# Perceiver block on one NeuronCore: the first batch's fill reordered, with matmuls on constants ahead of it

## The reference

```python
x = x + cross_attention(layernorm(x), ctx, ctx)      # 16 heads of 32, ctx is 8 x 512 x 512
x = x + linear_attention(layernorm(x))               # feature map elu+1, 128 features
x = x + moe(layernorm(x))                            # 16 experts, 8 tokens each per batch, and a shared one
```

```python
qh = (q @ Wq + bq).reshape(b, n, H, HD)
kh = (k @ Wk + bk).reshape(b, k.shape[1], H, HD)
vh = (v @ Wv + bv).reshape(b, v.shape[1], H, HD)
attn = jax.nn.softmax(scale * einsum("blhe,bshe->bhls", qh, kh), axis=-1)
out = einsum("bhls,bshd->blhd", attn, vh).reshape(b, n, H * HD) @ Wo + bo
```

## Time and profile before

| | |
|---|---|
| median of 3 runs | 668.30 us |
| lowest and highest | 667.94, 669.22 us |
| profiled execution, its own time | 668.04 us |
| its span, first to last instruction | 665.2 us |
| instructions in the span | 10401 |

### The profile page before, as it was taken

One profiled execution on the slowest core, in us unless ns is written; L12 is line 12 of the kernel. 1 busy time (PEld: TensorE's weight loads), 2 busy tenths in 40 slices (PEclk: granted clock), 3 DMA queues, 4 the chain that ended last, 5 costly groups with the idle time before them and its releaser, 6 DMA issues.

```text
span 665.2 us, 10401 instructions
## 1 busy us (share of the span) xinstructions
PE 638.2 (96%) x4216; PEld 414.6 (62%) x4216; DVE 312.3 (47%) x643; ACT 255.3 (38%) x488; POOL 34.8 (5%) x38
## 2 busy tenths in 40 slices
PE   6989999999999999999999988999999999999997
PEld 5767777777878786678978564444444434443433
DVE  5965636444453615755778675423223222323123
ACT  5645636444544536546684342111121212211210
POOL 0400000000000001535000000000000000000000
PEclk9999999999999999999999989999999999999999
DMA  8211010110340000031239724989999999999971
GB/s 314 82 64 64 2 65 2 63 53 12 125 194 0 2 1 2 1 111 34 98 108 399 283 97 165 379 356 396 391 414 414 403 403 401 394 379 397 372 282 70
DMA packets 14347, 129.55 MB, mean 195 GB/s; under 512 B 2720, under 2 KB 2848, under 8 KB 6240
## 3 DMA queue, kind: packets, MB, share of 16 engines
q1 hardware_dynamic: 12576, 127.15, 48.9%
q10 hardware_dynamic: 1728, 1.77, 0.8%
HBM read 125.90 MB, written 1.05 MB: 191 GB/s over the span
## 4 chain that ended last, share of the span: by engine, by line
PE 75%; DVE 9%; DMA 9%; ACT 4%; issue 2%; SPq 1%; DVEq 0%; ACTq 0%
PE ps L1209 23%; PE ps L1496 14%; DMA w_u<-in_wu 8%; PE ps L1533 7%; PE ps L1403 5%; PE ps L1506 4%; PE ps L1279 4%; PE ps L1546 3%; PE ps L1255 3%; PE ps L1290 2%; PE ps L1320 2%; PE ps L1450 2%; PE ps L1352 2%; PE ps L1462 1%; PE ps L1522 1%
## 5 line engine op out<-in xcount | busy, mean ns | idle before, releaser
L1496 PE MATMUL ps<-w_u,x_slot 128*64 128x512 f32 x256 | 58.1, 595 | 2.0 <-DMA w_u<-in_wu 2.0
L1496 PE MATMUL ps<-w_g,x_slot 128*64 128x512 f32 x256 | 58.1, 595 | 0.8 <-ACT x_slot L780 0.8
L1533 PE MATMUL ps<-w_d,hid_T 128*64 128x512 f32 x256 | 58.1, 596 | 0.7 <-issue 0.7
L582 ACT ACTIVATE probs<-ps,neg_max 128x512 f32<-128x512 f32 x64 | 43.5, 688 | 39.1 <-DVE neg_max L899 39.1
L742 ACT ACTIVATE hid<-ps 128x512 f32<-128x512 f32 x24 | 14.4, 598 | 102.5 <-PE ps L1496 76.8
L1209 PE MATMUL ps<-wv_hi,ctx_hi 128*128 128x512 f32 x128 | 51.6, 403 | 0.0
L1209 PE MATMUL ps<-wv_lo,ctx_hi 128*128 128x512 f32 x128 | 50.0, 390 | 0.0
L1209 PE MATMUL ps<-wv_hi,ctx_lo 128*128 128x512 f32 x128 | 49.8, 389 | 0.0
L879 DVE COPY probs_T<-ps 128x512 f32<-128x512 f32 x28 | 19.4, 692 | 64.8 <-PE ps L1279 64.8
L899 DVE TENSOR_REDUCE neg_max<-ps 128x1 f32<-128x512 f32 x64 | 39.7, 682 | 18.4 <-PE ps L1255 18.3
L1071 DVE TENSOR_TENSOR hid<-hid,ps 128x512 f32<-128x512 f32 x24 | 16.5, 687 | 65.8 <-PE ps L1496 36.2
(11 more groups left out here) (246 smaller groups left out, 1185.2 us busy)
## 6 DMA issues: line engine op xcount, KB each, us to landing
w_u<-in_wu SPq DMA_DIRECT2D x16, 2048.0 KB, 16.4
w_d<-in_wd SPq DMA_DIRECT2D x16, 2048.0 KB, 12.8
w_g<-in_wg SPq DMA_DIRECT2D x16, 2048.0 KB, 13.7
ctx_raw<-in_ctx SPq DMA_DIRECT2D x7, 1024.0 KB, 4.8
w_qkv<-in_wqkv SPq DMA_DIRECT2D x1, 3072.0 KB, 15.3
ws_g<-in_wsg SPq DMA_DIRECT2D x1, 2048.0 KB, 7.8
ws_u<-in_wsu SPq DMA_DIRECT2D x1, 2048.0 KB, 7.9
ws_d<-in_wsd SPq DMA_DIRECT2D x1, 2048.0 KB, 21.3
```

What stands on the lines that cost most here:

```text
L582: act.activation(probs[:, p, :], bank(SCORE[p]), ACT.Exp, bias=neg_max[:, p:p + 1], scale=1.0, accum_out=row_sum[:, p:p + 1]).then_inc(exp ...
L1496: ins = pe.matmul(ps[64 * fh:64 * (fh + 1), dst, :], x_slot[:, e, dt, :], weights[e % 2][:, dt, BANK * fh:BANK * (fh + 1)], start=(dt == 0 ...
L1533: ins = pe.matmul(ps[64 * fh:64 * (fh + 1), 6 + side(n), :], hid_T[:, side(n), j, 64 * fh:64 * (fh + 1)], w_d[e % 2][:, KT * fh + j, :], s ...
```

## The change

- TensorE begins with 34 matmuls (`WARM`) of 128 columns on the constant `ones`, into a bank that is not read before it is written anew. They wait for the first four constants only.
- `first_keys` goes part by part: for each depth tile high x high of all four key tiles, then low weights x high context, then high weights x low context, each behind its own wait.
- `ln_transpose` moves into the middle of value tile 3.
- `project_q` goes part by part over all depth tiles, high x high first; tile 0 uses bank 6 instead of 3.
- TensorE's order becomes: query tiles 0, 1, 2, first score group, query tile 3, key tile 0 of batch 1, second score group; `step(1)` then starts with key tile 1.
- The counter `q_done` becomes two, one for each engine that takes query tiles out.
- ScalarE: a square root on a constant at the very start; key outputs ahead of the first square roots; high parts of the query weights in two halves, with value output 0 between; value output 1 behind the last roots; query output 2 ahead of the exponents.
- GpSimd's first row bias waits in addition for the second score group of batch 1 (`score_ps` 4).

```diff
@@ -278,7 +278,7 @@
         w_hi, w_split, wv_split, wq_split = sem("w_hi"), sem("w_split"), sem("wv_split"), sem("wq_split")
         ctx_hi_done, ctx_split = sem("ctx_hi_done"), sem("ctx_split")
         k_ps, k_done, v_ps, v_done = sem("k_ps"), sem("k_done"), sem("v_ps"), sem("v_done")
-        q_ps, q_done, bias_scaled = sem("q_ps"), sem("q_done"), sem("bias_scaled")
+        q_ps, q_done, bias_scaled = sem("q_ps"), [sem("q_done_act"), sem("q_done_dve")], sem("bias_scaled")
         score_ps, max_done, exp_done, inv_done, prob_done = (
             sem("score_ps"), sem("max_done"), sem("exp_done"), sem("inv_done"), sem("prob_done"))
         pT_ps = sem("pT_ps")
@@ -316,7 +316,8 @@
         SCORE = (5, 6, 7, 2, 5, 6, 7, 3)
         GROUP = PAIRS // 2
         FIRST_K = 4
-        Q_BANK = (3, 4, 0, 1)
+        Q_BANK = (6, 4, 0, 1)
+        WARM = 34
 
         LN_BANK, RES_BANK = 2, ((7, 0, 1, 7), (0, 1, 2, 3))
         ROW_BANK = 4
@@ -494,6 +495,7 @@
                     pool.tensor_tensor(x[:, t, :], x[:, t, :], row_bias[:], ALU.add).then_inc(xbias_done, 1)
 
             pool.wait_ge(rows_in, 16)
+            pool.wait_ge(score_ps, 4)
             add_row_bias(0, bo_rows)
 
             def weights_low(parts):
@@ -570,7 +572,7 @@
             def q_out(ht):
                 act.wait_ge(q_ps, ht + 1)
                 act.activation(q_T[:, ht, :], bank(Q_BANK[ht]), ACT.Identity,
-                               bias=bias_q_scaled[:, ht:ht + 1], scale=HD ** -0.5).then_inc(q_done, 1)
+                               bias=bias_q_scaled[:, ht:ht + 1], scale=HD ** -0.5).then_inc(q_done[0], 1)
 
             def probs_T_out(b, tiles=range(KT)):
                 for ht in tiles:
@@ -589,30 +591,35 @@
                         if i >= 2:
                             v_out(b, 2 * g + i - 2)
 
+            def query_weights_high(tiles):
+                act.wait_ge(wq_in, 16)
+                for dt in tiles:
+                    act.copy(wq_hi[:, dt], wq_raw[:, dt]).then_inc(w_hi, 1)
+
+            act.wait_ge(consts, 4)
+            act.activation(newton[:, 0:1], iota_p[:], ACT.Sqrt)
             first_high()
             act.wait_ge(wv_in, 16)
             for dt in range(KT):
                 act.copy(wv_hi[:, dt], wv_raw[:, dt]).then_inc(w_hi, 1)
             act.wait_ge(bias_in, 48)
-            ln_std(0, (0, 1))
-            act.wait_ge(wq_in, 16)
-            for dt in range(KT):
-                act.copy(wq_hi[:, dt], wq_raw[:, dt]).then_inc(w_hi, 1)
             for ht in range(KT):
                 k_out(0, ht, first=True)
+            ln_std(0, (0, 1))
+            query_weights_high((0, 1))
+            act.wait_ge(wv_split, KT)
+            v_out(0, 0)
+            query_weights_high((2, 3))
             ln_std(0, (2, 3))
-            act.wait_ge(wv_split, KT)
-            for st in range(NS - 1):
-                v_out(0, st)
+            v_out(0, 1)
+            v_out(0, 2)
             xn_high()
             v_out(0, NS - 1)
             ctx_high(1, 1)
             act.wait_ge(bias_scaled, 1)
             q_out(0)
-            for p in range(GROUP - 1):
-                exponent(0, p)
             q_out(2)
-            for p in range(GROUP - 1, PAIRS):
+            for p in range(PAIRS):
                 exponent(0, p)
 
             def step(b, par, more=True):
@@ -871,7 +878,7 @@
             def q_out(ht):
                 dve.wait_ge(q_ps, ht + 1)
                 dve.tensor_scalar(q_T[:, ht, :], bank(Q_BANK[ht]), bias_q[:, ht:ht + 1], HD ** -0.5,
-                                  ALU.add, ALU.mult).then_inc(q_done, 1)
+                                  ALU.add, ALU.mult).then_inc(q_done[1], 1)
 
             def probs_T_out(b, tiles=range(KT)):
                 for ht in tiles:
@@ -1201,10 +1208,12 @@
                     ins = pe.transpose(ps[:, t, P * dt:P * (dt + 1)], xn_lin[:, t, P * dt:P * (dt + 1)], ident[:])
                 ins.then_inc(xnT_ps, 1)
 
-            def product3(dst, lhs, rhs):
+            def product3(dst, lhs, rhs, behind=None):
 
                 (l_hi, l_lo), (r_hi, r_lo) = lhs, rhs
                 for dt in range(KT):
+                    if behind and dt == KT // 2:
+                        behind()
                     for i, (a, c) in enumerate(((l_hi, r_hi), (l_hi, r_lo), (l_lo, r_hi))):
                         ins = pe.matmul(dst, a(dt), c(dt), start=(dt == 0 and i == 0), stop=(dt == KT - 1 and i == 2))
                 return ins
@@ -1212,15 +1221,14 @@
             def first_keys():
 
                 for dt in range(KT):
-                    pe.wait_ge(w_split, dt + 1)
-                    pe.wait_ge(ctx_split, dt + 1)
-                    for ht in range(KT):
-                        cols = slice(P * ht, P * (ht + 1))
-                        for i, (w, c) in enumerate(((wk_hi, ctx_hi), (wk_hi, ctx_lo), (wk_lo, ctx_hi))):
+                    for i, (w, c) in enumerate(((wk_hi, ctx_hi), (wk_lo, ctx_hi), (wk_hi, ctx_lo))):
+                        pe.wait_ge(*((ctx_hi_done, dt + 1), (w_split, dt + 1), (ctx_split, dt + 1))[i])
+                        for ht in range(KT):
+                            cols = slice(P * ht, P * (ht + 1))
                             ins = pe.matmul(bank(FIRST_K + ht), w[:, dt, cols], c[:, 0, dt, :],
                                             start=(dt == 0 and i == 0), stop=(dt == KT - 1 and i == 2))
-                        if dt == KT - 1:
-                            ins.then_inc(k_ps, 1)
+                            if dt == KT - 1 and i == 2:
+                                ins.then_inc(k_ps, 1)
 
             def project_k(b, par, tiles=range(KT)):
                 pe.wait_ge(ctx_split, b + KT)
@@ -1234,7 +1242,7 @@
                              (lambda dt: wk_hi[:, dt, cols], lambda dt: wk_lo[:, dt, cols]),
                              (lambda dt: ctx_hi[:, par, dt, :], lambda dt: ctx_lo[:, par, dt, :])).then_inc(k_ps, 1)
 
-            def project_v(b, par, st, first=False):
+            def project_v(b, par, st, first=False, behind=None):
                 if st >= 2:
                     pe.wait_ge(v_done, b * NS + st - 1)
                 elif first:
@@ -1244,7 +1252,7 @@
                 cols = slice(P * st, P * (st + 1))
                 product3(bank(PROJ[st % 2]),
                          (lambda dt: ctx_hi[:, par, dt, cols], lambda dt: ctx_lo[:, par, dt, cols]),
-                         (lambda dt: wv_hi[:, dt, :], lambda dt: wv_lo[:, dt, :])).then_inc(v_ps, 1)
+                         (lambda dt: wv_hi[:, dt, :], lambda dt: wv_lo[:, dt, :]), behind).then_inc(v_ps, 1)
 
             def score_group(b, g):
 
@@ -1302,40 +1310,43 @@
                 attend(b, 2)
                 attend(b, 3)
 
+            pe.wait_ge(consts, 4)
+            for _ in range(WARM):
+                pe.matmul(ps[:, LN_BANK, 0:P], ones[:], ones[:], start=True, stop=True)
             pe.wait_ge(consts, HPT + 5)
             first_keys()
             for st in range(NS - 1):
                 project_v(0, 0, st, first=True)
             pe.wait_ge(k_done, 2)
-            ln_transpose()
-            project_v(0, 0, NS - 1, first=True)
+            project_v(0, 0, NS - 1, first=True, behind=ln_transpose)
 
             def project_q(ht):
                 cols = slice(P * ht, P * (ht + 1))
-                for dt in range(KT):
-                    if ht == 0:
-                        pe.wait_ge(wq_split, dt + 1)
-                        pe.wait_ge(xn_split, dt + 1)
-                    for i, (w, c) in enumerate(((wq_hi, xn_hi), (wq_hi, xn_lo_cross), (wq_lo, xn_hi))):
+                for i, (w, c) in enumerate(((wq_hi, xn_hi), (wq_lo, xn_hi), (wq_hi, xn_lo_cross))):
+                    for dt in range(KT):
+                        if ht == 0:
+                            pe.wait_ge(*((xn_hi_done, dt + 1), (wq_split, dt + 1), (xn_split, dt + 1))[i])
                         ins = pe.matmul(bank(Q_BANK[ht]), w[:, dt, cols], c[:, dt, :],
                                         start=(dt == 0 and i == 0), stop=(dt == KT - 1 and i == 2))
                 ins.then_inc(q_ps, 1)
 
-            pe.wait_ge(xn_split, 2)
+            pe.wait_ge(k_done, KT)
             project_q(0)
             project_q(1)
-            pe.wait_ge(k_done, KT)
-            pe.wait_ge(q_done, 2)
-            score_group(0, 0)
             pe.wait_ge(v_done, NS)
             project_q(2)
+            for done in q_done:
+                pe.wait_ge(done, 1)
+            score_group(0, 0)
+            pe.wait_ge(q_done[0], 2)
             project_q(3)
-            pe.wait_ge(q_done, KT)
+            project_k(1, 1, (0,))
+            pe.wait_ge(q_done[1], 2)
             pe.wait_ge(exp_done, GROUP - 1)
             score_group(0, 1)
 
             def step(b, par):
-                project_k(b, par, range(KT - 1))
+                project_k(b, par, range(b == 1, KT - 1))
                 probs_transpose(b - 1, 0)
                 probs_transpose(b - 1, 1)
```

## The result

The changed kernel takes **671.45 us** (median of 5 runs, 670.98 to 672.67) against 667.94 for the kernel before in the same comparison (666.49 to 669.22, 5 runs). The ratio is 1.0064, 95% interval 1.0047 to 1.008: slower by 0.6%, where 667.3 was forecast and "faster" had the highest chance (0.48). The profiled execution's span is 670.6 us, 5.4 more than before; it was the second slowest of the five (672.55), so its trace shows somewhat more loss than the median does.

The account below looks back on a forecast made before the run. TensorE, busy 96% of the span, was taken as the bound, with time to win in batch 0's fill. Fill gain -2.5 plus clock fall +1.5 gave -1.0: 668.04 to 667.0 profiled, median 0.3 higher, 667.3; range 664.9 to 669.4.

Parts of the forecast that it names:

- The first keys: Batch 0's key products at the start: after the warm-up they end at 17.4 instead of 18.55, -1.15 us.
- if the clock rises 3.5 us in, as before: TensorE's warm-up: 19 matmuls at 0.178 us, then 15 at 0.11, 5.0 us in all, ending at 6.5.
- Rival D: Slower: the warm-up matmuls do not raise the clock, keys end at 20.2, 670.1 us; chance 0.14.
- the chain from the keys' end on: Fill from value tile 0 (17.4) to batch 1's third key tile: 52.1 against 54.57, a gain of 2.5 us.
- the gap and its price: TensorE before batch 1's third key tile: 3.3 us idle, then a clock fall costing +1.5 us.
- rival B: The clock holds over the idle gap before batch 1's third key tile, 665.8 us; chance 0.24.
- The row that the prediction drew on: Granted clock 0.50 at 389 us after idles of 1.01 and 0.77 us, used to expect a fall after 3.3 us.
- delays the scores by the rest: Key tile 0 before the second scores: of its 2.73 us, 0.84 covers idle and the rest delays those scores.
- the row bias: GpSimd's additions moved away: VectorE's low query weights take 2.5 us, not 5.69; additions near 72 us cost nothing.
- the Exp table load: ScalarE's 1.28 us load moves behind query output 2; first exponent 0.4 us late, second score group's wait hidden.
- Rival C: Short warm-up ending at 5.2, keys end at 16.1, value weights bind; 666.0 us with the clock fall, 664.5 without; chance 0.10.

Follow-up runs that it names:

- run 1: The changed kernel without the 34 warm-up matmuls: 667.45 us, ratio 0.9994 to the kernel before.
- Run 8: The kernel before with only GpSimd's row bias held back until the second scores of batch 1: 666.97 us, ratio 0.9976.
- run 2: The changed kernel with 8 matmuls of 512 columns on constants in place of the 34 of 128: 665.78 us, ratio 0.997 to the kernel before.
- run 3: The kernel before with only the 34 warm-up matmuls put ahead: 669.91 us, ratio 1.0033.
- run 4: The changed kernel with the 3 MB weight load held back until batch 5's scores are done: 670.37 us, ratio 1.0041 to the kernel before.
- Run 6: The changed kernel with 8 wide warm-up matmuls and 13 unread matmuls in the gap before batch 1's third key tile: 664.22 us, ratio 0.9944.
- run 5: The changed kernel with 8 wide warm-up matmuls and batch 1's key tile 0 behind the second scores: 664.22 us, ratio 0.9947 to the kernel before.
- run 9: The changed kernel with 8 wide warm-up matmuls, key tile 0 behind second scores, 16 transposes in the gap, query output 3 before two normalisations: 662.49 us, ratio 0.9931.
- run 10: The kernel before with only 8 warm-up matmuls of 512 columns put ahead: 667.69 us, ratio 1.0001.

## Why the prediction was wrong, point by point

**The step that failed is the first term,** "The first keys: -1.15". Its price of 0.178 us for a warm-up matmul at the low clock was taken from four transposes; it was 0.215, which makes 1.2 us over the 34. And its condition, "if the clock rises 3.5 us in, as before", did not hold: it rose only after 512-column key products had run, which makes another 2.5: 0.9 in the warm-up itself and 1.6 in the slow key products. Value tile 0 came at 21.12 instead of 17.4, an error of 3.7 us. The "as before" was also the short end of what the kernel does: in runs 1 and 8, without a warm-up, the clock rose some 5.5 us behind the first product. Rival D had the outcome, that these matmuls do not raise the clock; it was given 0.14 and its warm-up was priced 1.0 us too short, with keys at 20.2 and 670.1 us. Its reason, the weight loading, was not tested. Runs 1 to 3 show the cost from both sides: taken out, the time falls by 0.7%; put on the kernel before, it rises by 0.33%. Both figures contain the hole of the next paragraph. Run 2 shows the cause, since only the kind and number of the matmuls differ.

**Not in the prediction at all: the hole at 192 us,** 1.7 us. No term and no rival asked what 34 more instructions do to the rest of TensorE's program. Runs 1 to 4 tie it to the instructions and the load together. The four single profiles bear this out, and the ratio of run 4 (1.0041 against 1.0064) agrees in size, though their intervals overlap.

With the two, the sum comes out: 668.3 - 1.0 + 3.7 + 1.7 = 672.7. The median was 671.45, the profiled execution, from which the two were read, 672.55.

**Right: the chain from the keys' end on.** From value tile 0 to the third key tile the forecast had 34.7 us (52.1 - 17.4) and the trace has 35.05, against 36.02 before. The transposes lie 9.52 us behind value tile 0 (9.55 forecast). Of the 0.35 that are missing some 0.2 are pace: a query product takes 0.232 us and not 0.227, and there are 36 ahead of the first scores (33.78 to 42.23).

**Right: the gap and its price.** 3.10 us of idle (3.3 forecast), then the low clock, 1.58 us (1.5). Run 6 shows the price alone at 1.6 to 1.7; rival B, that the clock holds, fell. The Trainium skill's warning against idle gaps between bursts of matmuls (TensorE: Matmul & The Clock Gate, "Why this matters for your kernels") agrees with the trace here: 3.10 us of idle, then a granted clock of 0.50. The row that the prediction drew on was weaker than it looked: the same idles of some 1.0 and 0.77 us in the expert stage are followed by no fall at that place in the profiles of runs 3, 5 and 6, so they alone do not make it fall. The remark that key tile 0 "delays the scores by the rest" of its 2.73 us, 1.9, holds with run 9: from the first to the second scores 4.94 us against 6.78 in run 2. In run 5 it was 5.60, since VectorE's query output stood behind two normalisations.

**Right: the row bias.** 5.69 us became 2.49, and the additions near 77.7 cost nothing visible. Run 8 gives -1.6 us for it alone, in a kernel where the query products waited for it. The stretch of a normalisation was up to 1.1 us rather than 0.8, on two of four.

**Right: the Exp table load.** It did move behind the query output (43.04) and was hidden: the second scores waited for it neither in the change nor in run 9.

**Rival C** (a short warm-up, value weights then bind) is what run 2 made come true: value tile 0 waits for the low value weights, which were ready at 17.4 and not at 16.02. The rival's time with the fall was 666.0; run 2 measured 665.78.

## What to carry to other kernels

Warm TensorE up with the kind of matmul that the kernel's own rows show at full clock, and see that it ends when the first operand arrives, so that no idle follows it (in run 10 a warm-up with 1.86 us of idle behind it brought nothing); price it at its own pace, not by something that looks like it. When a reorder takes work from behind a chain that ends in a wait, look what is left to fill that wait: the gap is paid twice, once as idle and once at half clock, and work moved into it (here 16 transposes, 0.9923) did better than filler (0.9944, with intervals that overlap). Instructions added at the start shift the whole program behind them, and can cost where nothing was changed. Before two single profiles are subtracted, their granted clocks have to be compared stretch by stretch.

## What the runs showed of the hardware

- 34 matmuls of 128 columns in one row, 0.215 us apart for 7.3 us, did not bring the 2.4 GHz level; full pace came 3.1 us (changed kernel) and 2.2 us (run 3) into the 512-column products that followed. Without a warm-up it came 3.5 us (before) to 5.7 us (run 1) into them. Behind eight of 512 columns in 3.8 us (run 2) it was there from the first products on.
- A hole of 1.5 to 1.7 us without any recorded wait, inside a group of 16 small matmuls, appeared in two kernels with 34 instructions more and a 3 MB load in flight, and in none of the other ten profiles.
- GpSimd's four additions take 6.67 us beside VectorE's subtractions of two SBUF operands and 5.23 beside maxima and normalisations. Row maxima out of PSUM were not stretched (2.48 us for four, as before); normalisations were.
- The fall of the clock in the expert stage (0.50 for some 3 us, between 384 and 412 us) is in nine of the twelve profiles and not in those of runs 3, 5 and 6. The times go with it: of the 32 executions of the kernel before that were timed beside runs 1 to 4, the 8 with a mean granted clock of 1.000 average 666.3 us and the 17 with 0.997 average 667.9.
